# Bias products as contiguous rows, and every engine's steps up to the first scores in another order, in a cross-attention block on one core

## What is computed

```python
q, kv = ln(x), ln(ctx)
qp, kp, vp = q @ Wq.T + bq, kv @ Wk.T + bk, kv @ Wv.T + bv
scores = qh @ kh.T / sqrt(32) - spatial_scale * dist(query_xy, token_xy) + spatial_offset
attn = softmax(where(mask, scores, -inf)) @ vh
x = x + attn @ Wo.T + bo
x = x + gelu(ln(x) @ W1.T + b1) @ W2.T + b2
```

## Time and profile before

| | us |
|---|---|
| runs: median (lowest to highest) | 1251.14 (1250.59 to 1253.05) |
| the profiled execution's own time | 1252.47 |
| its span, first to last instruction | 1250.6 |
| busy: PE, PEld | 1220.2, 819.0 |
| busy: DVE, POOL, ACT | 993.6, 992.0, 851.3 |

### The profile page before, as it was taken

One profiled execution on the slowest core, in us unless ns is written; L12 is line 12 of the kernel. 1 busy time (PEld: TensorE's weight loads), 2 busy tenths in 40 slices (PEclk: granted clock), 3 DMA queues, 4 the chain that ended last, 5 costly groups with the idle time before them and its releaser, 6 DMA issues.

```text
span 1250.6 us, 27744 instructions
## 1 busy us (share of the span) xinstructions
PE 1220.2 (98%) x9424; PEld 819.0 (65%) x9424; DVE 993.6 (79%) x2656; ACT 851.3 (68%) x1914; POOL 992.0 (79%) x1286
## 2 busy tenths in 40 slices
PE   9888988999999999999999999999999999999998
PEld 6656455666667666666666676666666666666664
DVE  5799998888878888888888989888888787778321
ACT  5867757676877677676767677776767677676331
POOL 5478897989898898989898998989898987767320
PEclk9788999999999999999999999999999999999999
DMA  6699999888999898998999998998889897879543
GB/s 185 197 188 208 224 224 195 192 189 209 209 194 222 180 214 198 193 203 201 198 205 218 180 223 182 202 203 203 194 206 208 195 208 176 173 170 180 142 113 123
DMA packets 468686, 241.69 MB, mean 193 GB/s; under 512 B 384048, under 2 KB 408896, under 8 KB 468544
## 3 DMA queue, kind: packets, MB, share of 16 engines
q1 hardware_dynamic: 468544, 239.91, 85.6%
HBM read 109.66 MB, written 12.58 MB: 98 GB/s over the span
## 4 chain that ended last, share of the span: by engine, by line
PE 86%; DVE 8%; issue 2%; ACT 1%; POOL 1%; DMA 1%; SPq 0%; POOLq 0%; DVEq 0%; ACTq 0%
PE ps_up L630 26%; PE ps_down L645 26%; PE ps_qk L566 12%; PE ps_vo L590 6%; PE ps_vo L587 6%; PE ps_s L601 5%; PE ps_pv L615 4%; DVE p_nat L1071 1%; DVE soft L1054 1%; PE ps_down L510 1%; DVE w L999 1%; DVE w L1005 1%; DVE x_nat L1031 1%; PE ps_down L541 0%; DVE qk_parts L1045 0%
## 5 line engine op out<-in xcount | busy, mean ns | idle before, releaser
L1248 POOL TENSOR_SCALAR p_nat<-soft,row_inv 128x256 f16<-128x256 f32 x512 | 332.1, 658 | 61.2 <-DVE row_inv L1065 59.4
L630 PE MATMUL ps_up<-hT,w 128*128 128x256 f16 x3072 | 377.2, 273 | 3.1 <-ACT u L805 2.7
L645 PE MATMUL ps_down<-w,hid 128*128 128x512 f16 x1536 | 372.9, 379 | 0.8 <-DVE hid L1103 0.4
L630 PEld LDWEIGHTS ps_up<-hT,w 128*128 128x128 f16 x3072 | 300.3, 98 | 93.2 <-ACT u L805 3.2
L773 ACT ACTIVATE soft<-soft,neg_max 128x256 f32<-128x256 f32 x512 | 255.2, 500 | 117.2 <-DVE neg_max L1054 116.2
L1054 DVE CUSTOM_DVE_ANT_0 soft<-ps_s,soft,factor 128x256 f32<-128x256 f32 x512 | 225.4, 476 | 116.7 <-PE ps_s L601 115.9
L1071 DVE SCALAR_TENSOR_TENSOR p_nat<-soft,row_inv,p_nat 128x256 f16<-128x256 f32 x512 | 297.6, 620 | 2.1 <-POOL p_nat L1248 1.9
L1256 POOL TENSOR_SCALAR soft<-dist,scale_neg,offset 128x512 f32<-128x512 f32 x256 | 244.3, 954 | 14.0 <-DVE p_nat L1071 13.6
L645 PEld LDWEIGHTS ps_down<-w,hid 128*128 128x128 f16 x1536 | 148.6, 97 | 132.4 <-DMA w<-x_scratch 1.4
L805 ACT ACTIVATE u<-ps_up,bias,up_scale 128x256 f32<-128x256 f32 x256 | 142.3, 556 | 124.9 <-PE ps_up L630 121.5
L1264 POOL TENSOR_SCALAR hid<-u,hid_scale 128x1024 f16<-128x1024 f32 x64 | 77.3, 1208 | 105.0 <-ACT u L811 105.0
(11 more groups left out here) (122 smaller groups left out, 1569.5 us busy)
## 6 DMA issues: line engine op xcount, KB each, us to landing
w<-x_scratch SPq DMA_DIRECT2D x256, 256.0 KB, 3.1
stack<-qk_parts SPq DMA_DIRECT2D x256, 96.0 KB
raw<-in_ctx SPq DMA_DIRECT2D x32, 256.0 KB, 3.4
raw<-in_x SPq DMA_DIRECT2D x32, 256.0 KB, 3.1
c_stage<-in_w SPq DMA_DIRECT2D x32, 256.0 KB, 3.6
x<-in_x SPq DMA_DIRECT2D x32, 256.0 KB, 3.5
out<-x SPq DMA_DIRECT2D x32, 256.0 KB, 3.2
tok_rows<-in_tok_xy SPq DMA_DIRECT2D x16, 256.0 KB, 4.4
```

What stands on the lines that cost most here:

```text
L630: mm = e.matmul(ps_up[s % 2][:, 0:L], w_1_sb[:, wp, k, m * P:(m + 1) * P], hT[:, b % 2, :, xp * KT + k, :], start=(k, wp, xp) == (0, 0, 0) ...
L645: mm = e.matmul(ps_down[tt][:], hid[:, chunk % HID_RING, i, hp, tt * P:(tt + 1) * P], w_2_sb[:, s % W2_RING, wp, :], start=(m == 0 and (hp ...
L1248: mine = e.tensor_scalar(p_nat[:, nat, HI, lc, :], soft[:, ring, lc, :], row_inv[:, ring, lc:lc + 1], 1.0, ALU.mult, ALU.mult)
```

## The change

The bias products are turned round: the shift's column is the stationary operand and 512 columns of the weights move, so four products give a whole section as one row of 512 values on one partition (`weight_bias`, and `w1_bias` one product a slot, the four chunks' rows on partitions 0, 32, 64 and 96, after `clear_rows` has written that bank once). ScalarE copies the row out in the order of the columns (`bias_row`, `bias_rows_1`), a DMA lays it over the partitions (`bias_turn`, `bias_turn_1`), and VectorE adds the given bias as before. The value section's products all stand in slot 0, `value_bias_out` in slot 5 instead of 4.

The steps of the opening get other slots on all engines: the query's total at -26 behind its products, the first token tiles' norms apart, the key's split in two halves before and after the query's gains, the two score factors and the scaling of small constants behind the query's split instead of in its gains and at -5, the distances at -5 instead of -22. The value's split moves on ScalarE from -3 to -1 and on VectorE from -3 to 0; the squares of the value and output weights from -6 and -2 to -4 and 0. All steps of w_1 and w_2 come one slot earlier. Warm-ups are 10, 1, 1, 14, 6, 8 instead of 10, 3, 10, 8, 2, 8; `keep_busy` starts at slot 0 (into the attention's bank below slot 9), and fills up to 14, where a bias product of w_1 counts 4 instead of 8.

```diff
+    TOTAL = (-30, -26, -3, 0) + tuple(range(0, 32, 4))
+    NORM = (-28, -24, -2, 0) + tuple(range(1, 33, 4))
+    GAIN = (-26, -22, -1, 1) + tuple(range(2, 34, 4))
+    ROW_K, ROW_Q, ROW_V, ROW_1 = 1, 2, 3, 4
...
+        def bias_turn(sec):
+            gate.wait_ge(s_row, AT[sec] + 1)
+            e.dma_start(bias_qkv[:, sec * KT:(sec + 1) * KT], (row_q if sec == SEC_Q else row_kv)[:]).then_inc(s_rowd[sec], DMA)
+        def bias_turn_1():
+            gate.wait_ge(s_row, ROW_1)
+            for c in range(N_CHUNKS):
+                e.dma_start(bias_1[:, c * CH:(c + 1) * CH], rows_1[32 * c:32 * c + 1, :]).then_inc(s_rowd_1, DMA)
...
-            gate.wait_ge(s_mkept, DMA)
-            gate.wait_ge(s_colsum, 1)
+            if t >= KT:
+                gate.wait_ge(s_rowd_1, N_CHUNKS * DMA)
...
+            for sec, at_slot in ((SEC_K, -26), (SEC_Q, -19), (SEC_V, 2)):
+                if slot == at_slot:
+                    bias_turn(sec)
+            if slot == 18:
+                bias_turn_1()
...
-            for s in due(slot, 21, ITEM, MT):
+            for s in due(slot, 20, ITEM, MT):
                 store_w2(s)
-            if slot == DOWN - 1:
-                load_w2(0)
-            for s in due(slot, DOWN - 1, ITEM, N_STEPS - 1):
-                load_w2(s + 1)
+            for s in due(slot, DOWN - 2, ITEM, N_STEPS):
+                load_w2(s)
...
-            for step in due(slot, -5, ITEM, 2 * N_CHUNKS * KT):
+            for step in due(slot, -6, ITEM, 2 * N_CHUNKS * KT):
...
-        def weight_bias(sec, quarters):
+        def weight_bias(sec):
...
             b_ln = B_Q if sec == SEC_Q else B_KV
-            for k in quarters:
-                gate.wait_ge((s_wk if sec == SEC_K else s_wq)[k], DMA)
-                for m in range(KT):
-                    col = sec * KT + m
-                    mm = e.matmul(ps_bias[sec][:, col:col + 1], w_stage[sec][:, k, m * P:(m + 1) * P],
-                                  cols_sb[:, b_ln + k:b_ln + k + 1], start=((k, m) == (0, 0)), stop=((k, m) == (KT - 1, KT - 1)))
-            if KT - 1 in quarters:
-                mm.then_inc(s_brow)
-        def value_bias(m):
-            sec, b_ln = SEC_V, B_KV
-            gate.wait_ge(s_w[0], DMA)
-            gate.wait_ge(s_cols, DMA)
-            gate.wait_ge(s_bcol, BIAS_Q)
-            col = sec * KT + m
+            if sec == SEC_V:
+                gate.wait_ge(s_row, ROW_K)
             for k in range(KT):
-                mm = e.matmul(ps_bias[sec][:, col:col + 1], w_stage[sec][:, k, m * P:(m + 1) * P],
-                              cols_sb[:, b_ln + k:b_ln + k + 1], start=(k == 0), stop=(k == KT - 1))
-            if m == KT - 1:
-                mm.then_inc(s_brow)
-        def w1_bias(c, m):
-            col = c * CH + m
-            for k in range(KT):
-                gate.wait_ge(s_wc[c % C_STAGES][k], n_staged(c))
-                mm = e.matmul(ps_bias_1[:, col:col + 1], staged(c, k)[:, m * P:(m + 1) * P],
-                              cols_sb[:, B_M + k:B_M + k + 1], start=(k == 0), stop=(k == KT - 1))
-            if m == CH - 1:
+                if sec == SEC_V:
+                    gate.wait_ge(s_w[0], DMA)
+                else:
+                    gate.wait_ge((s_wk if sec == SEC_K else s_wq)[k], DMA)
+                mm = e.matmul(ps_bias[sec][0:1, :], cols_sb[:, b_ln + k:b_ln + k + 1], w_stage[sec][:, k, :],
+                              start=(k == 0), stop=(k == KT - 1))
+            mm.then_inc(s_brow)
+        def w1_bias(c, k):
+            gate.wait_ge(s_wc[c % C_STAGES][k], n_staged(c))
+            mm = e.matmul(ps_bias_1[32 * c:32 * c + 1, :], cols_sb[:, B_M + k:B_M + k + 1], staged(c, k),
+                          start=(k == 0), stop=(k == KT - 1))
+            if k == KT - 1:
...
+        def clear_rows():
+            e.matmul(ps_bias_1[:], w_sec[SEC_K][:, HI, 0, 0:P], w_sec[SEC_K][:, HI, 0, :], start=True, stop=True)
...
+        def keep_busy(bank, count):
+            if bank is ps_down[0]:
+                gate.wait_ge(s_bo_all, 1)
+            gate.wait_ge(s_wlo, AT[SEC_K] + 1)
...
-                e.matmul(ps_down[0][:], w_sec[SEC_K][:, HI, 0, 0:P], w_sec[SEC_K][:, HI, 0, :], start=True, stop=True)
+                e.matmul(bank[:], w_sec[SEC_K][:, HI, 0, 0:P], w_sec[SEC_K][:, HI, 0, :], start=True, stop=True)
...
-        SLOT_STEPS = 16
+        SLOT_STEPS = 14
...
-            for at_slot, count in ((-32, 10), (-30, 3), (-8, 10), (-6, 8), (-3, 2), (-2, 8)):
+            for at_slot, count in ((-32, 10), (-30, 1), (-26, 1), (-8, 14), (-6, 6), (-2, 8)):
...
-            for sec, quarters, at_slot in ((SEC_K, range(3), -31), (SEC_K, range(3, KT), -29), (SEC_Q, range(1), -29),
-                                          (SEC_Q, range(1, 3), -28), (SEC_Q, range(3, KT), -27)):
+            for sec, at_slot in ((SEC_K, -31), (SEC_Q, -29), (SEC_V, 0)):
                 if slot == at_slot:
-                    weight_bias(sec, quarters)
-            for m, at_slot in enumerate((-2, 0, 2, 2)):
-                if slot == at_slot:
-                    value_bias(m)
-            if slot == 4:
+                    weight_bias(sec)
+            if slot == 0:
+                clear_rows()
+            if slot == 5:
                 value_bias_out()
...
-            if 7 <= slot < DOWN:
+            if 0 <= slot < DOWN:
                 taken = 1 + (3 if due(slot, 9, GROUP, N_HG) else 0) + (6 if slot % 2 else 0) + (6 if slot >= UP else 0)
-                taken += vo_done + (8 if due(slot, 1, ITEM, MT) else 0)
-                keep_busy(max(0, SLOT_STEPS - taken))
+                taken += vo_done + (4 if due(slot, 1, ITEM, MT) else 0)
+                taken += 16 if slot in (0, 5) else 0
+                keep_busy(ps_pv if slot < 9 else ps_down[0], max(0, SLOT_STEPS - taken))
...
+        def quarter_squares(sec, quarters):
+            for k in quarters:
...
-            gate.wait_ge(s_bcol, BIAS_Q)
+            gate.wait_ge(s_row, ROW_Q)
...
+        def by_column(row):
+            return row.rearrange("p (q m) -> p m q", m=KT)
+        def bias_row(sec):
+            gate.wait_ge(s_brow, AT[sec] + 1)
+            if sec == SEC_V:
+                gate.wait_ge(s_rowd[SEC_K], DMA)
+            e.activation(by_column((row_q if sec == SEC_Q else row_kv)[:]), ps_bias[sec][0:1, :].rearrange("p (m q) -> p m q", m=KT), ACT.Copy).then_inc(s_row)
+        def bias_rows_1():
+            gate.wait_ge(s_brow, 3 + N_CHUNKS)
+            gate.wait_ge(s_mkept, DMA)
+            gate.wait_ge(s_colsum, 1)
+            e.activation(by_column(rows_1[0:97, :]), ps_bias_1[0:97, :].rearrange("p (m q) -> p m q", m=KT), ACT.Copy).then_inc(s_row)
...
+            gate.wait_ge(s_gs, GAINED_Q if sec == SEC_Q else GS[AT[sec]])
...
+            gate.wait_ge(s_rowd[SEC_Q], DMA)
...
-            for sec, at_slot in ((SEC_K, -25), (SEC_Q, -20), (SEC_V, -3)):
+            for sec, at_slot in ((SEC_K, -29), (SEC_Q, -24), (SEC_V, 1)):
+                if slot == at_slot:
+                    bias_row(sec)
+            if slot == 17:
+                bias_rows_1()
+            for sec, at_slot in ((SEC_K, -26), (SEC_Q, -20), (SEC_V, -1)):
                 if slot == at_slot:
                     weight_hi(sec, range(KT))
             for half_of in due(slot, 1, ITEM, 2):
                 weight_hi(SEC_O, range(2 * half_of, 2 * half_of + 2))
-            for sec, at_slot in ((SEC_K, -31), (SEC_Q, -30)):
+            for sec, quarters, at_slot in ((SEC_K, range(KT), -31), (SEC_Q, range(2), -30), (SEC_Q, range(2, KT), -29)):
                 if slot == at_slot:
-                    quarter_squares(sec)
-            for sec, at_slot in ((SEC_V, -6), (SEC_O, -2)):
+                    quarter_squares(sec, quarters)
+            for sec, at_slot in ((SEC_V, -4), (SEC_O, 0)):
...
-                if slot == -22:
+                if slot == -5:
...
-            for step in due(slot, -3, ITEM, 2 * N_CHUNKS * KT):
+            if slot == -4:
+                dist_sqrt(0)
+            for step in due(slot, -4, ITEM, 2 * N_CHUNKS * KT):
                 chunk_square(*divmod(step, KT))
-            for step in due(slot, 3, ITEM, MT):
+            for step in due(slot, 2, ITEM, MT):
                 w1_hi(*divmod(step, KT))
-            for s in due(slot, 19, ITEM, MT):
+            for s in due(slot, 18, ITEM, MT):
                 w2_hi(s)
             for chunk in due(slot, UP + CH - 1, CH, B * N_CHUNKS):
                 mlp_gelu(chunk)
-            if slot == -4:
-                dist_sqrt(0)
...
+        def score_factors():
+            key, query = slice(AT[SEC_K], AT[SEC_K] + 1), slice(AT[SEC_Q], AT[SEC_Q] + 1)
+            e.scalar_tensor_tensor(out=factor[:, 0:1], in0=norm[:, query], scalar=-SCORE_SCALE / A_SCALE ** 2,
+                                   in1=norm[:, key], op0=ALU.mult, op1=ALU.mult).then_inc(s_gs)
+            e.scalar_tensor_tensor(out=factor[:, 1:2], in0=inv[:, query], scalar=A_SCALE ** 2 / SCORE_SCALE,
```

(44 more changed lines are left out.)

31 lines of the change are left out of this document (9 added, 22 removed).

## The result

The kernel after took 1255.59 us (median of 7 runs, 1254.67 to 1258.26), beside 1251.14 us for the kernel before (7 runs, 1249.44 to 1253.43). The ratio is 1.0033, with a 95% interval of 1.0020 to 1.0046: slower, by more than the measurement leaves open. The forecast was 1251.1 with 1246 to 1256 as its range.

A forecast was written before the change was run, and what follows sets the result against it. TensorE bounds the kernel from 207.5 us, VectorE from 66.5 to 176. +2.8 - 0.7 - 2.7 = -0.6, or +0.6 with the clock fallen: 1252.5 us profiled, 1.3 above the median, so 1251.1; range 1246 to 1256.

The forecast's parts named there:

- The opening: Up to the stack copies: row products bring the query's sum 3.9 us earlier; 4.4 us won, 3.2 with the clock fallen.
- Rival C: Opening: one-column stationary products do not raise the clock, so the query's sum comes later; +5.8, 1257 us, chance 0.14.
- Slot 0: Chain from the output weights' square over total and value split to scores(2): 4.4 us won become 4.0 lost.
- B: Rival: the slot 0 chain costs VectorE only what it costs today; -4.4, 1246.7 us, chance 0.27.
- Slots 1 to 31: Between the opening slots and the handover: the loss shrinks from 4.0 to +2.8 at slot 7 and +2.1 at slot 31.
- The wait of VectorE for the output bias: By slot 7: this wait of 1.21 us goes, as its products stand one slot earlier than their reader.
- 0.7 come back with the clock: By slot 31: fillers from slot 0 keep the clock up and return 0.7 us; bounds 0 and 2.7.
- cancels: By slot 7: the first chunk's norm already done and one more piece of w_1 done earlier offset each other.
- Rival E: Early slots: the low clock holds the slots and the fillers lift it; 17.3 us, 1234 us, chance 0.02.
- The handover: Slots 31 to 36: fewer fillers and earlier w_2 pieces give back 2.7 us; bounds 0.5 and 3.4.
- D: Rival: the handover gives back 0.5 instead of 2.7, another wait taking the place; 1253.8 us, chance 0.15.
- The steady stretch: From 207.5 to 1224 us: TensorE is busy 1016.49 of 1016.50 us, and its length stays unchanged.

The follow-up runs named there:

- e10: Before with the row form of the bias products alone, old step order, value bias steps one slot later: 1252.93 us, ratio 1.0000.
- e8: After with 27 warm-up products instead of 1 ahead of the query's total: 1262.15 us, ratio 1.0072.
- e7: Before with a filling level of 14 instead of 16 TensorE products a slot from slot 7: 1250.27 us, ratio 0.9983.
- e1: After with the square of the output weights moved back from slot 0 to slot -2: 1255.18 us, ratio 1.0020.
- e3: After with the output weights' square in slot -2 and the value split directly behind maximum 0, ahead of the wait for the total: 1251.10 us, ratio 0.9994.
- e9: After with the output weights' square in slot -2, value split directly behind maximum 0, and value bias spread, product and reader one slot earlier: 1249.57 us, ratio 0.9973.
- e4: After with all steps of w_1 and w_2 one slot later, as before has them: 1259.90 us, ratio 1.0065.
- e6: Before with all steps of w_1 and w_2 one slot earlier: 1254.01 us, ratio 1.0006.
- e5: After with its fillers from slot 7 on instead of from slot 0: 1256.74 us, ratio 1.0042.
- e12: After with before's filling level, 16 instead of 14, in slots 31 to 36 alone: 1256.62 us, ratio 1.0032.

## Why the prediction was wrong

On the profiled pair the forecast was -0.6 to +0.6, and +2.2 came. Point by point:

**The opening** held in direction and was undersized. The query's total came 5.5 us earlier instead of 3.9 (14.10 against 19.63), since the row products ran at full clock from the first on, where I had let it rise in their middle. Rival C is refuted by the rows at 6.08 and 10.13 and by e10, where the clock rose within them (last section). C's own price was too high by its condition: it charges all 6.4 us though the first 2 are to decide nothing, and e8 lost 1.7 of 5.7 on the way. The stack copies went out 4.7 us earlier (4.4 forecast). Of before's 19.63 a part is its execution: in e7 the same instructions bring the total at 17.86.

**Slot 0** held up to maximum 2: VectorE waits for the total, then splits, and maximum 2 is 4.6 us late where 4.0 were forecast; e1 to e3 take the chain away link by link, and refute B. I had not seen that the second key copy on ScalarE waits for the landing of the stack copies (2.04 us at 35.95), and by these rows only 2.5 of the opening's win are left at maximum 0, nor that the value projection would run at half clock (L595, six products in 2.74 us where I had 1.3); before's own row for it, 2.72 us at 43.97, would have told me.

**Slots 1 to 31** is the step that failed. "The wait of VectorE for the output bias (1.21 us) goes" and 0.7 come back with the clock: 1.9 us less. What came is 0.6 more, +4.6 to +5.2. Three things make up the 2.5 us (1.2, 0.7 and 0.7).

The chain of slot 0 did not end at maximum 2. From maximum 2 to 3 after takes 6.32 us and before 5.15, 1.2 more where I had nothing. VectorE waits 0.64 us for the upper halves of two output pieces, which ScalarE makes behind the value products of TensorE, and its two rows take 2.17 us; in before the same two stand without a wait:

```profile
52.75 1.40 DVE L989 SCALAR_TENSOR_TENSOR w_o<-w_stage,factor,w_o 128x512 f16<-128x512 f32 x2
```

With the chain taken away this stretch takes 4.83 us (e3) and 4.84 (e9).

The wait did not go, it moved. The products of the value bias with the output weights stand one slot later in the kernel than before, and the third piece of w_1 one slot earlier; this piece waits 1.67 us for exactly these products. I had moved the reader (`bias_out`) and looked whether it still waits, and had booked the early piece of w_1 as work that "cancels" without asking what it waits for. From maximum 3 to 7 after is 0.5 us shorter than before where 1.2 were forecast. e9 undoes it and is 0.9 shorter.

The 0.7 from the clock did not come: from maximum 7 to 31 after takes 101.86 us and before 101.89, at a clock of 0.97 and 0.92. Rival E is refuted in the same place.

**The handover** gave 4.0 instead of 2.7, beyond my upper bound of 3.4: the mechanism is the one forecast (e4, e6), and D is refuted. This hid half of the failure of the step before. The versions with the same handover took 35.82 to 36.66 us for it, and after stands at the short end, so I would not carry the 4.0 as a constant.

**The steady stretch** took 1.4 us more in after from maximum 40 to 255 (932.77 against 931.37), in which I had forecast nothing. In after's trace TensorE has two stops of 1.0 us together there that wait for nothing shown, and none in before's. In the other versions it took 931.1 to 933.3, with the same instructions in all. I can't say from one profile each whether that belongs to the kernel; it stays open.

**The sum**: +0.6 in slot 0, +2.5 in slots 1 to 31, -1.3 in the handover and +1.0 behind it are +2.8, which leads from -0.6 to +2.2. The medians differ by 4.45. The forecast carried the 1.3 us by which before's profile stood above its median over to after, whose profile stands 0.9 on the other side; that is the other 2.2 us of the difference, and no row shows where they arise.

The Trainium skill (TensorE: Matmul & The Clock Gate, "What's actually happening") has the engine throttled by default and released by activity. The rows agree: in e10 the clock rose behind ten warm-up products and within the row products, and in after the six value products at 49.82, behind 3.13 us of idle time, ran at half clock.

## What to carry to other kernels

When a producer is moved later and another step earlier, list for each instruction that now stands earlier what it waits for; a wait whose own reader moved away is often taken over by the next one that waits for the same products. In a stretch where one engine has no slack, a wait that moves is not a wait that goes, and a long piece of that engine's own work (here the split of the value weights) is best placed ahead of the place at which it must wait. And where an edit moves steps by one slot at both ends of a pipeline, look at both: in before the shift of the w_1 and w_2 steps (e6) cost 7.5 us by maximum 31 and gave back 3.1 in the handover. And before a difference in the clock is credited to an edit, look whether the edited instructions stand ahead of it: the row that spoke for the early fillers in e5 stood ahead of the first filler.

## What the runs showed of the hardware

A product with a single stationary column and 512 float32 moving ones runs as fast as a full one: eight records in 3.59 us, 0.43 apart, and in after (L549) eight with a full stationary in 3.60.

```profile
70.38 3.60 PE L549 MATMUL ps_down<-w_stage,bias_v 128*128 128x512 f32 x8
```

These row products hold the full clock, and it can rise within them. In before and in e10 the ten warm-up products at 1.52 us took 4.45 us alike. Behind them before has its products of one moving column, and the three warm-ups that follow at 11.29 us still take 1.44 us; e10 has the row products, and the same three take 0.82 (TensorE of e10):

```profile
5.90 3.06 PE L531 MATMUL ps_down<-w_stage,cols 128*1 128x512 f32 x6
8.89 0.82 PE L665 MATMUL ps_pv<-attnT 128*128 128x512 f16 x3
```

In e7, which has before's instructions here, the clock had already risen (the warm-ups took 3.83 us), and it fell within the products of one moving column: 24 of their records took 3.70 us where before has 5.25, and the three warm-ups behind them took 1.44 again. Where the clock stands at a given instruction can differ between two executions of the same instructions; after and e12 show it at the projection of slot 1 (1.48 and 2.18 us).

ScalarE's copy of one partition of 512 float32 elements from PSUM in column order takes 1.06 us (x3, 1.056 to 1.072), more than a 128 x 512 copy in straight order (0.60 to 0.71 us), and so more than the 0.6 I took. The query's copy stood ahead of 1.05 us of idle time. The value row's copy at 51.20 us stands directly ahead of two output pieces, for which VectorE then waits 0.37 us.
